# Fp4 feed-forward of a four-layer network: second buffer for the gated values, other PSUM banks, and a new order of norm, division and addition

## What is computed

```
def fp4_quant_dequant(x):
    xb = x.reshape(shape[:-1] + (shape[-1] // BLOCK, BLOCK))
    scale = jnp.max(jnp.abs(xb), axis=-1, keepdims=True) / 6.0
    scale = jnp.maximum(scale, jnp.float32(1e-12))
    xn = xb / scale
    idx = jnp.searchsorted(_MID, jnp.abs(xn))
    q = _GRID[idx] * jnp.sign(xn) * scale
    return q.reshape(shape)
def fp4_linear(x, w):
    xq = fp4_quant_dequant(x)
    wq = fp4_quant_dequant(w)
    return jnp.einsum('bsk,nk->bsn', xq, wq)
gate = fp4_linear(x, w_gate)
y = fp4_linear(x, w_up)
h = jax.nn.silu(gate) * y
return fp4_linear(h, w_down)
```

## Time and profile before

| | |
|---|---|
| timed runs (us) | 2069.52, 2079.42, 2080.34; median 2079.42 |
| the profiled execution | 2071.99, its span 2070.1 |
| busy in the span | PE 1803.5 (87%), DVE 1292.1 (62%), ACT 1042.6 (50%), POOL 713.1 (34%) |
| the fp4 stage, 416 to 598 us | 182.0, of which DVE busy 127.9, PE 105.9, POOL 84.7, ACT 35.5; granted clock 0.77 |

### The profile page before, as it was taken

The page is one execution under the profiler, slowest core; times in us unless marked ns, Lnnn a source line. Parts: engine busy times, 40 slices in busy tenths (PEclk is TensorE's granted clock), DMA queues, the critical chain, the costliest instruction groups (busy, mean ns, idle before and its releaser), DMA issues.

```text
span 2070.1 us, 33125 instructions
## 1 busy us (share of the span) xinstructions
PE 1803.5 (87%) x11885; PEld 811.1 (39%) x11885; DVE 1292.1 (62%) x3442; ACT 1042.6 (50%) x1768; POOL 713.1 (34%) x796
## 2 busy tenths in 40 slices
PE   4888888656559999998999999999999957999998
PEld 1233333234424444444445443233333234444443
DVE  3777777367767777771111114999999537766663
ACT  1566666412116666663223221888888834454432
POOL 4476776535442223201011012222223036444420
PEclk9899999768869999998999998999999969999999
DMA  5453222000024322400000010333222010000000
GB/s 132 114 139 80 62 67 58 1 17 1 0 61 107 80 63 64 113 11 3 0 0 1 0 49 13 85 88 76 63 63 62 2 51 1 6 6 6 6 11 11
DMA packets 67963, 91.68 MB, mean 44 GB/s; under 512 B 10924, under 2 KB 61340, under 8 KB 62924
## 3 DMA queue, kind: packets, MB, share of 16 engines
q1 hardware_dynamic: 66072, 89.04, 18.1%
q10 hardware_dynamic: 1728, 0.53, 0.2%
HBM read 49.30 MB, written 39.85 MB: 43 GB/s over the span
## 4 chain that ended last, share of the span: by engine, by line
PE 52%; issue 5%; DVE 3%; ACT 3%; DMA 2%; SPq 1%; POOL 1%; DVEq 0%; ACTq 0%; POOLq 0%
PE ps L1442 5%; PE ps L412 5%; PE ps L1454 5%; PE ps L386 4%; PE ps L2885 3%; PE ps L1419 3%; PE ps L2155 3%; PE ps L398 3%; PE ps L2157 2%; PE ps L2173 2%; PE ps L370 2%; PE ps L332 2%; DMA Qst<-mT 2%; PE ps L354 1%; PE ps L1848 1%
## 5 line engine op out<-in xcount | busy, mean ns | idle before, releaser
L702 DVE TENSOR_REDUCE mx<-ps 128x1 f32<-128x512 f32 (+3 forms) x1024 | 534.1, 582 | 108.3 <-PE ps L354 80.0
L600 ACT ACTIVATE Pr<-ps 128x1024 f32<-128x1024 f32 (+3 forms) x512 | 348.0, 706 | 179.3 <-PE ps L337 92.3
L593 ACT ACTIVATE Pr<-ps 128x512 f32<-128x512 f32 x512 | 275.3, 601 | 44.2 <-PE ps L386 37.4
L354 PE MATMUL ps<-Kst,Qst 63*128 63x512 bf16 (+3 forms) x1024 | 221.9, 315 | 55.2 <-DVE mx L702 29.4
L698 DVE CUSTOM_DVE_ANT_0 vs<-ps,cT 128x512 f32<-128x512 f32 (+3 forms) x512 | 225.8, 488 | 61.5 <-PE ps L354 58.0
L332 PE MATMUL ps<-Qst,Kst 64*128 64x512 bf16 (+3 forms) x1024 | 221.8, 310 | 16.9 <-ACT Pr L600 8.4
L2913 POOL TENSOR_TENSOR ve<-mv,eps 128x4 f32<-128x4 f32 x41 | 8.8, 215 | 577.3 <-DVE mv L2902 577.3
L370 PE MATMUL ps<-Pr,V 128*32 128x512 f32 (+3 forms) x2048 | 198.3, 460 | 6.4 <-ACT ctxU L606 2.9
L398 PE MATMUL ps<-Kst,Qst 63*128 63x512 bf16 x512 | 172.7, 404 | 5.5 <-DVE mx L702 3.3
L412 PE MATMUL ps<-Pr,V 128*32 128x256 f32 x2048 | 164.5, 393 | 8.5 <-ACT ctxU L606 7.6
L386 PE MATMUL ps<-Qst,Kst 64*128 64x512 bf16 x512 | 157.6, 388 | 9.7 <-DMA Qst<-mT 5.7
(11 more groups left out here) (340 smaller groups left out, 3272.1 us busy)
## 6 DMA issues: line engine op xcount, KB each, us to landing
Qst<-parts_scratch SPq DMA_DIRECT2D x48, 384.0 KB, 6.4
Kst<-parts_scratch SPq DMA_DIRECT2D x48, 384.0 KB, 8.4
parts_scratch<-qpart SPq DMA_DIRECT2D x24, 384.0 KB, 2.7
parts_scratch<-kpart SPq DMA_DIRECT2D x24, 384.0 KB, 3.2
parts_scratch<-qpart SPq DMA_DIRECT2D x24, 256.0 KB, 2.9
parts_scratch<-kpart SPq DMA_DIRECT2D x24, 256.0 KB, 3.3
parts_scratch<-qpart SPq DMA_DIRECT2D x24, 128.0 KB, 2.8
parts_scratch<-kpart SPq DMA_DIRECT2D x24, 128.0 KB, 3.3
```

The costliest lines, as they stand in the source:

```text
L354: mm = pe.matmul(ps[:, 4 + a, lo:lo + W], k.Qst[rows, n.par, pair, P * it:P * it + P], k.Kst[rows, n.par, pair, 0:W], start=True, stop=True)
L593: act.activation(k.Pr[:, g % 2, 2 * (j // 2) + 1 - j % 2, :], ps[:, self.bank_t(b, g, j), :], ACT.Exp).then_inc(self.s_exp.sem, 1)
L600: act.activation(k.Pr[:, g % 2, 2 * tile:2 * tile + 2, 0:W], ps[:, 2 * tile:2 * tile + 2, 0:W], ACT.Exp).then_inc(self.s_exp.sem, 1)
L702: dve.tensor_reduce(k.mx[:, half, at:at + 1], ps[:, bank, lo:lo + W], AX_X, ALU.max, negate=True).then_inc(self.s_max.sem, 1)
```

## The change

In words:

- h gets two buffers, by the batch's parity. The gated products of f+1 wait for the division of batch f-1 instead of batch f.
- `hq` moves into the memory of the divided h, `quant_f[0]`. So GpSimd's division of batch f, which writes there, waits for the transposes of h of batch f-1 on TensorE; the store of h no longer waits for the down products.
- PSUM: four banks for up products (3, 4, 0, 2), one (bank 1) for all gates and for the turn. All four up products of a batch now stand beside its gates in `first`, and `rest` is gone; each gate waits for the silu of the one before.
- VectorE: `norm_stats` ahead of the scale of h; the addition ahead of the long passes instead of behind them.
- GpSimd: the norm ahead of the division of h.

```diff
-        self.h, self.hq, = (flat[:, j * NT * self.PAD:(j + 1) * NT * self.PAD].rearrange("p (t c) -> p t c", t=NT)
-                            for j in range(2))
...
+        wide = NT * self.HID
+        self.h = [flat[:, j * wide:(j + 1) * wide].rearrange("p (t c) -> p t c", t=NT) for j in range(2)]
+        self.hq = k.quant_f[0][:, T:T + wide + self.PAD - self.HID]
...
-    TURN, GATE, UP, HT, OUT = 0, 1, 3, 5, 7
+    GATE, UP, HT, OUT = 1, (3, 4, 0, 2), 5, 7
...
-            pe.wait_ge(self.s_gate.sem, self.s_gate.at(n, t - 1))
-            pe.matmul(ps[:, self.GATE + t % 2, 0:self.HID], k.xT[:, n.par, P * t:P * t + P],
+            pe.wait_ge(self.s_gate.sem, self.s_gate.at(n, t))
+            pe.matmul(ps[:, self.GATE, 0:self.HID], k.xT[:, n.par, P * t:P * t + P],
...
-            pe.wait_ge(self.s_h.sem, self.s_h.at(n, t - 1))
-            pe.matmul(ps[:, self.UP + t % 2, 0:self.HID], k.xT[:, n.par, P * t:P * t + P],
+            pe.wait_ge(self.s_h.sem, self.s_h.at(n.plus(-1), t + 1))
+            pe.matmul(ps[:, self.UP[t], 0:self.HID], k.xT[:, n.par, P * t:P * t + P],
...
             if n.c > 1:
-                self.turn(pe, n, ps[:, self.TURN, :])
-            gate(n, 0)
-            up(n, 0)
-            gate(n, 1)
-            up(n, 1)
-            gate(n, 2)
-            gate(n, 3)
-
-        def rest(n):
-            up(n, 2)
-            up(n, 3)
+                pe.wait_ge(self.s_gate.sem, self.s_gate.at(n.plus(-1)))
+                self.turn(pe, n, ps[:, self.GATE, :])
+            for t in range(NT):
+                gate(n, t)
+                up(n, t)
...
             if f.valid():
                 down(f)
-            if later.valid():
-                rest(later)
...
-                    dve.wait_ge(self.q_h.s_v.sem, self.q_h.s_v.at(n.plus(-1)))
-                dve.tensor_tensor(self.h[:, t, 0:self.HID], ps[:, self.UP + t % 2, 0:self.HID],
+                    dve.wait_ge(self.q_h.s_v.sem, self.q_h.s_v.at(n.plus(-2)))
+                dve.tensor_tensor(self.h[n.par][:, t, 0:self.HID], ps[:, self.UP[t], 0:self.HID],
...
             if f.valid():
+                k.norm_stats(dve, later, self)
                 quantize(self.q_h, f, 0)
             if f.c == NB - 1:
                 self.after.open_split(dve)
-            if f.valid():
-                k.norm_stats(dve, later, self)
...
             if f.valid():
-                quantize(self.q_h, f, 1)
                 if f.c > 0:
                     add(f.plus(-1))
+                quantize(self.q_h, f, 1)
...
             if f.valid():
+                k.norm_apply(pool, later, self, self.q_x.s_v, 2)
+                pool.wait_ge(self.s_hT_ps.sem, self.s_hT_ps.at(f.plus(-1)))
                 self.q_h.gpsimd(pool, f, 0)
-                k.norm_apply(pool, later, self, self.q_x.s_v, 2)
...
             if f.valid():
-                self.q_h.gpsimd(pool, f, 1, self.s_out_ps)
+                self.q_h.gpsimd(pool, f, 1)
```

More of the change, by code:

```diff
@@ L1070, in prepare @@
         rows, b16 = "p (t b c) -> p t b c", Quantizer.BLOCK
-        self.h, self.hq, = (flat[:, j * NT * self.PAD:(j + 1) * NT * self.PAD].rearrange("p (t c) -> p t c", t=NT)
-                            for j in range(2))
-        self.gate = [k.ctxU, k.ctxT, flat[:, 2 * NT * self.PAD:2 * NT * self.PAD + self.HID],
-                     flat[:, 2 * NT * self.PAD + self.HID:2 * NT * self.PAD + 2 * self.HID]]
+        wide = NT * self.HID
+        self.h = [flat[:, j * wide:(j + 1) * wide].rearrange("p (t c) -> p t c", t=NT) for j in range(2)]
+        self.hq = k.quant_f[0][:, T:T + wide + self.PAD - self.HID]
+        self.gate = [k.ctxU, k.ctxT, flat[:, 2 * wide:2 * wide + self.HID],
+                     flat[:, 2 * wide + self.HID:2 * wide + 2 * self.HID]]
         self.hT = [k.vs[:, 0, :], k.vs[:, 1, :], k.tile(13)]
@@ L1085, in prepare @@
         cut = lambda t: t[:, :, 0:self.HID].rearrange("p t (b c) -> p t b c", c=b16)
-        self.q_h = Quantizer(k, "fq_h", (NT, self.HID // b16, b16), lambda n: cut(self.h),
-                             lambda n: cut(self.hq), T)
-    TURN, GATE, UP, HT, OUT = 0, 1, 3, 5, 7
+        self.q_h = Quantizer(k, "fq_h", (NT, self.HID // b16, b16), lambda n: cut(self.h[n.par]),
+                             lambda n: self.hq[:, 0:NT * self.HID]
+                             .rearrange("p (t b c) -> p t b c", t=NT, c=b16), T)
+    GATE, UP, HT, OUT = 1, (3, 4, 0, 2), 5, 7
     EARLY = ((0, 4, 4), (4, 4, 5), (8, 1, 4))
@@ L1209, in down @@
                     mm = pe.transpose(ps[:, self.HT + kt % 2, P * t:P * t + P],
-                                      self.hq[:, t, P * kt:P * kt + P], k.ident[:, :])
+                                      self.hq[:, self.HID * t + P * kt:self.HID * t + P * kt + P], k.ident[:, :])
                 mm.then_inc(self.s_hT_ps.sem, 1)
@@ L1223, in frame @@
                 first(nxt)
-                rest(nxt)
             if later.valid():
@@ L1256, in gates @@
                 act.wait_ge(self.s_h.sem, self.s_h.at(n.plus(-1), t + 1))
-                act.activation(self.gate[t][:, 0:self.HID], ps[:, self.GATE + t % 2, 0:self.HID], ACT.Silu)\
+                act.activation(self.gate[t][:, 0:self.HID], ps[:, self.GATE, 0:self.HID], ACT.Silu)\
                    .then_inc(self.s_gate.sem, 1)
@@ L1265, in frame @@
                 if f.valid():
-                    self.turned(act, later, ps[:, self.TURN, :])
+                    self.turned(act, later, ps[:, self.GATE, :])
                 gates(later)
@@ L1291, in vector @@
         ps = k.ps
-        dve.memset(self.hq[:, :, self.HID:self.PAD], 0.0).then_inc(self.s_pad.sem, 1)
+        dve.memset(self.hq[:, NT * self.HID:], 0.0).then_inc(self.s_pad.sem, 1)
         def gated(n):
```

## The result

The changed kernel took 2065.46 us (median of 7 runs, 2058.97 to 2067.93), the kernel before in the same comparison 2075.93 us (7 runs, 2069.52 to 2080.34). The ratio is 0.9945 with a 95% interval of 0.9932 to 0.9957, or 11.4 us less, 9 to 14. It was measured again beside the last experiments: 0.9932, 0.9912 to 0.9952. The forecast was 2066.4 us and 13.0 us less.

A forecast was written before the change was run, and what follows sets the result against it. VectorE's frame was taken to bound the fp4 feed-forward, with its exclusion against GpSimd as second limit. Frames 1 to 5 -11.5, frame 0 -1.8, frames 6 and 7 +0.3 give -13.0 us: 2079.42 to 2066.4, range 2053 to 2077.

The forecast's parts named there:

- The frame: Fp4 feed-forward, one long L1033's end to the next: 21.71 us falls to 19.4, saving 11.5 over frames 1 to 5.
- The scale of x: VectorE's small operation, excluded by GpSimd's division of h until 8.65 us into the frame: about 1.2 us of new wait.
- The transposes: TensorE's transposes of h end at 5.6, GpSimd wants them at 5.95; late in one frame of three or four, adding 0.2.
- TensorE's row of products: All eight products of x ahead of the transposes of h, through one gate bank: 6.9 us, ending at 3.6.
- the ring without the wait: VectorE's frame beside GpSimd's chain, before adding 0.2 for late transposes: 19.2 us, 2.5 less than 21.71.
- Rival 1: TensorE's longer row of products paces the frame: frames of 20.0 to 20.4, 7.5 us less, 2072; chance 0.2.
- Frame 0: First frame of the stage: 1.8 us less, bounded by 0 and -3, first gates through one bank costing 0.8 to 1.0.
- Frames 6 and 7: Last frames: frame 6 paced by TensorE, change 0; frame 7 +0.3 us, between -1 and +2.
- The other reading: Main rival of the experiments' theory: 3.8 us of waits per frame removed (1.66 + 2.12), each part worth its wait.
- Rival 2: TensorE's clock stays low through the whole burst, GpSimd's division waits for transposes: 8 us more, 2088; chance 0.05.
- Rival 3: More is gained, clock may not fall and small operations may cross GpSimd's free: frames 18.5, 2060; chance 0.13.
- Rival 4: Waits return elsewhere, exclusion costs 1.5 us more per frame: frames of 20.9, 5 us less, 2074; chance 0.12.

The follow-up runs named there:

- c2: Kernel with the quantized h in the third quantizer buffer, with GpSimd's division of x moved ahead of its division of h: frames 1 to 5 19.72 us, stage 175.0.
- b3: Changed kernel with the quantized h in the third quantizer buffer instead of the first: frames 1 to 5 18.75 us, stage 166.5, one timed run 2054.25.
- c3: Changed kernel once more, unaltered: 2062.63 us, ratio 0.9932 to the kernel before; frames 1 to 5 19.26 us, stage 171.6.
- a3: Changed kernel with the old PSUM banks, third and fourth up products behind the down products: frames 1 to 5 21.64 us, stage 179.6.
- b4: Changed kernel with two gate banks for the first two batches alone: frame 0 ends at 25.4 us, frames 1 to 5 19.15, stage 168.7.
- b1: Kernel before with two buffers of h, and hq in the third quantizer buffer to make room: frames 1 to 5 21.71 us, stage 181.9.
- b2: Kernel before with the new PSUM bank plan alone: frames 1 to 5 20.43 us, stage 180.7.
- a4: Changed kernel with one buffer of h again: frames 1 to 5 22.10 us, stage 184.7.
- a2: Changed kernel with the norm again behind the division of h, on VectorE and GpSimd: frames 1 to 5 23.66 us, stage 196.6.
- a1: Changed kernel with the addition again behind the long passes over h: frames 1 to 5 19.25 us, stage 170.6.

## Why the prediction was right

**The total** came out close in part by luck. In the stage the forecast was 13.0 us less and the profiles have 13.3, but the terms differ more: frames 1 to 5 -12.1 instead of -11.5, frame 0 -0.55 instead of -1.8, frame 6 +0.15 instead of 0, frame 7 -0.5 instead of +0.3, the end -0.3 instead of 0. The predicted time of 2066.4, 0.9 from the median measured, also starts from a median of three runs (2079.42) that is 3.5 above that of seven (2075.93), while the saving between the medians of seven is 10.5 and not 13.0.

**The frame** was its main term, and its mechanism held: 19.4 forecast (19.2 and 0.2 for late transposes), 19.28 and 19.26 measured. All three steps of it can be seen. GpSimd's chain sets the start of x's quantizer. The scale of x was to wait about 1.2 us; it took 2.21, 2.05, 0.18, 1.62 and 2.16 us in frames 1 to 5, as the division of h, waiting for the transposes, started later in four of them. (1.62 is the frame without that wait; in the one with 0.18 the division started so late that the stall fell on the next operation.) The long L1026 was forecast at 1.5 and took 1.36, L1028 at 0.90 and took 0.89. c2 shows that the exclusion is the cause, not only a fit.

**The transposes** were given 0.35 us of slack and one late frame in three or four, 0.2 us on the mean. Without the wait a frame is 18.75 (b3), so it costs 0.53 on the mean; it stood in four frames of five, and in three of five in c3. The step that was too small is TensorE's row of products: 6.9 us forecast, 7.5 in the frame shown. The transposes, forecast to end at 5.6, ended at 472.69 - 466.40 = 6.3 there. GpSimd's norm, forecast at 5.95, ended at 5.93.

The error was hidden by one of the other sign: the ring without the wait was taken as 19.2, 0.45 too long. Three terms carry that. The division was to end 8.65 us after the long pass; in b3 it ends 8.47 after it (472.93 - 464.46), which is 0.18. The other two are the stalled operations, in b3:

```profile
471.40 1.57 DVE L1017 TENSOR_SCALAR fq_x_scale<-fq_x_amax 128x32 f32<-128x32 f32 x1
...
477.60 1.36 DVE L1026 TENSOR_SCALAR f_shared<-f_shared 128x1408 int32<-128x1408 int32 x1
```

The scale of x ends at 472.97, 0.04 after the division, and the long L1026 at 478.96, 0.75 after the store of x (477.16 + 1.05). The prediction let each start when GpSimd ended and then take its whole 0.18 or 0.89, which is 0.14 too much twice. Its own reading of L1028 (ended 0.75 after GpSimd, 0.90 alone) already had this. Rival 1 was thus partly true all along, at half its price, and the sign that the prediction named for it, GpSimd idle ahead of L1038 for the transposes, did appear.

**Frame 0** was mis-sized: 1.8 us less were forecast, 0.55 came. The single gate bank behind the table load was priced at 0.8 to 1.0; a3 (25.5) and b4 (25.4) against 27.9 show 2.4 to 2.5. The price was made of the wait alone, and left out that TensorE's granted clock then stays at 0.50 for some 3.5 us more (the two stretches under b4).

**Frames 6 and 7.** Frame 6: 0 forecast, +0.15 and +1.5 in two profiles, a scatter by TensorE's clock that the prediction had not given it. Frame 7: +0.3 forecast, -0.5 measured. The terms that the prediction names for it don't give +0.3: the addition +0.6 and the norm -1.5 are -0.9, with the split's stall the same. And the addition costs nothing there, since the interval already held one (the L1307 at 568.58, which has moved ahead as well). Measured are -1.6 for the old stalls of the long passes (1.76 and 2.35 us instead of 0.89 and 1.62), +0.7 for a second stalled operation of the split (L260, 1.15 instead of 0.43), and +0.4 for the scale of h beside the centring.

**The other reading, part by part,** is refuted. By it the second buffer is worth 1.7, the banks 2.1. Alone they are worth 0.0 (b1) and 1.3 (b2); taken out of the changed kernel they cost 2.8 (a4) and 2.4 (a3), the norm's place 4.4 (a2), the addition's nothing (a1). About half of the gain in the frames comes with the banks alone; the rest comes only when the parts stand together.

**Rival 2,** slower by a clock that stays low, did not come, but its place was right: the wait of the division for the transposes is the changed kernel's weak point. **Rival 3** (frames of 18.5) is what b3 comes near, by another way. **Rival 4** (the exclusion costs 1.5 us more per frame) is out: the frames of b3, which have the stalls and not the wait, are shorter than forecast. What stays open is why the clock of TensorE rose 4.7 us into its last burst in one profile of the changed kernel and 8.0 us into it in the other, with the same instructions; no run here was made for it.

## What to carry to other kernels

Draw the ring of two or three engines before pricing a wait: what a removed wait is worth is set by what is late next, and a buffer that frees one place may add nothing alone. When a buffer is moved into the memory of another tensor, the wait that this makes belongs where its producer was done long ago: here one line further (a third buffer) turned 0.4 to 1.05 us of waiting per frame into none. And an elementwise instruction of 0.2 us on VectorE can take 2 us when it stands beside a long one on GpSimd; look for it in the durations, since no list of waits has it.

## What the runs showed of the hardware

- Two forms of VectorE's `tensor_scalar` in SBUF waited for a running `tensor_tensor` of GpSimd to its end: fp32 128x32 took 2.05 us (changed kernel), int32 128x512 2.79 (c2), against 0.18 and 0.43 alone. The maximum (1.59 us), the norm's statistics (0.86), and products with one operand in PSUM (0.46 to 0.51) stood beside GpSimd's operations too and did not wait. It shows as a longer instruction, not as idle time, so the wait list doesn't have it.
- A stalled instruction ended sooner after GpSimd's than it takes alone: 0.04 us instead of 0.18 (128x32, b3), 0.28 instead of 0.43 (128x512, c2), 0.75 instead of 0.89 (128x1408, b3).
- In the kernels where TensorE paused for 0.8 us near the start of its work, its clock rose 7.4 to 9.6 us after L796 instead of 3.6 to 5.6. With the pause itself that cost 2.4 to 2.5 us (a3 and b4 against the changed kernel).
- In b3 and c2 the five frames agree within 0.03 us (18.75 to 18.76, 19.71 to 19.74), while the changed kernel's took 18.81 to 19.64. In this stage the scatter of the frames came from the engine with a varying clock: it went when TensorE left the ring.
